# Eight start addresses, 64 bytes apart, for the stationary operands of two neighbouring routed tiles

## The reference

```python
h = jnp.einsum('bct,bcd->bdt', x, weights[subjects]) + bias[subjects][:, :, None]
h = h.reshape(-1, 512)                      # 4096 tokens
logits = h @ gate_weight.T                  # 16 experts in 4 groups of 4
# the best 2 groups, in them the best 4 experts; weights normalised, times 2.5
def body(acc, inp):
    g, u, d, we = inp                       # g, u: (256, 512)   d: (512, 256)
    y = silu(h @ g.T) * (h @ u.T) @ d.T
    return (acc + we[:, None] * y, None)
out, _ = jax.lax.scan(body, jnp.zeros_like(h), (gate_proj, up_proj, down_proj, cw.T))
shared = silu(h @ shared_gate.T) * (h @ shared_up.T) @ shared_down.T
return x + (out + shared).reshape(64, 64, 512)
```

## Time and profile before

| | us |
|---|---|
| median of 3 runs | 827.67 |
| lowest and highest run | 824.30, 828.04 |
| span of the profiled execution, first to last instruction | 823.5 |
| TensorE busy in it (4133 matmuls) | 811.2 |
| TensorE's share of the chain that ended last | 93% |

### The profile page before, as it was taken

One profiled execution on the slowest core, in us unless ns is written; L12 is line 12 of the kernel. 1 busy time (PEld: TensorE's weight loads), 2 busy tenths in 40 slices (PEclk: granted clock), 3 DMA queues, 4 the chain that ended last, 5 costly groups with the idle time before them and its releaser, 6 DMA issues.

```text
span 823.5 us, 19365 instructions
## 1 busy us (share of the span) xinstructions
PE 811.2 (99%) x4133; PEld 650.1 (79%) x4134; DVE 484.7 (59%) x1017; ACT 389.1 (47%) x782; POOL 434.8 (53%) x399
## 2 busy tenths in 40 slices
PE   9999999999999999999999999999999999999996
PEld 5567878888887788888888888888888888888874
DVE  5788899626544445644457446747557466464441
ACT  4864434435343445544346445546455355453441
POOL 5503111525567555566655655755665674765543
PEclk9999999999999999999999999999999999999999
DMA  8986967899999999899997999899998998998965
GB/s 301 395 320 176 249 148 220 221 219 270 235 251 233 182 188 190 189 286 239 185 198 187 280 216 206 209 264 187 244 264 170 285 245 203 235 207 176 194 80 69
DMA packets 145305, 181.52 MB, mean 220 GB/s; under 512 B 30570, under 2 KB 103922, under 8 KB 142834
## 3 DMA queue, kind: packets, MB, share of 16 engines
q0 software_dynamic: 37776, 89.08, 52.6%
q1 hardware_dynamic: 106528, 80.45, 37.8%
q10 hardware_dynamic: 834, 10.49, 3.7%
HBM read 82.52 MB, written 67.17 MB: 182 GB/s over the span
## 4 chain that ended last, share of the span: by engine, by line
PE 93%; DMA 3%; DVE 1%; issue 1%; ACT 0%; DVEq 0%; POOLq 0%; POOL 0%; SPq 0%; ACTq 0%
PE psGU L1111 47%; PE psY L1111 23%; PE psY L1169 5%; PE psH L982 4%; PE psGU L1152 4%; PE psGU L1154 4%; PE psGU L1153 4%; DMA x_ring<-x_pairs 2%; DMA raw_w<-ffn_w 1%; PE psT L982 1%; PE psM L1139 1%; PE psGU L1031 1%; PE psH L1008 0%; DMA cond_sb<-cond_w 0%; DVE split_w L1340 0%
## 5 line engine op out<-in xcount | busy, mean ns | idle before, releaser
L1111 PE MATMUL psGU<-split_w,xT_pair 128*128 x1716 | 414.2, 390 | 0.9 <-issue 0.9
L1111 PEld LDWEIGHTS psGU<-split_w,xT_pair 128*128 128x128 f32 x1716 | 321.8, 188 | 70.1 <-issue 1.8
L694 POOL DMA_INDIRECT out<-y_ring,idx_all x143 | 227.2, 1589 | 202.0 <-SPq L583 183.1
L1758 DVE SCALAR_TENSOR_TENSOR aT<-aT,w_ring,psGU 128x256 f32<-128x256 f32 x143 | 68.6, 480 | 238.0 <-ACT aT L934 217.3
L689 POOL DMA_INDIRECT tok_ring<-h_rows,idx_all x143 | 152.2, 1064 | 72.7 <-issue 42.1
L1111 PE MATMUL psY<-split_w,hidT_hi 128*128 x564 | 187.4, 413 | 0.0
L934 ACT ACTIVATE aT<-psGU 128x256 f32<-128x256 f32 x143 | 55.0, 385 | 253.9 <-PE psGU L1111 253.9
L840 ACT ACTIVATE y_ring<-psY 128x512 f32<-128x512 f32 x173 | 103.6, 599 | 99.7 <-PE psY L1111 62.3
L1111 PE MATMUL psY<-split_w,hidT_lo 128*128 x282 | 111.1, 394 | 0.0
L1111 PEld LDWEIGHTS psY<-split_w,hidT_hi 128*128 128x128 f32 x564 | 95.4, 189 | 12.6 <-issue 0.2
L1743 DVE STREAM_TRANSPOSE psT<-x_ring 128x512 f32<-128x512 f32 x143 | 102.6, 717 | 2.3 <-DMA w_ring<-tok_ring 2.3
(11 more groups left out here) (268 smaller groups left out, 652.8 us busy)
## 6 DMA issues: line engine op xcount, KB each, us to landing
x_ring<-tok_ring SPq DMA_DIRECT2D x284, 128.0 KB
raw_w<-ffn_w SPq DMA_DIRECT2D x17, 1536.0 KB, 9.8
out<-y_ring POOLq DMA_DIRECT2D x32, 256.0 KB, 10.6
x_ring<-x_pairs SPq DMA_DIRECT2D x12, 512.0 KB, 8.3
h_rows<-tok_ring SPq DMA_DIRECT2D x16, 256.0 KB, 9.6
h_rows<-y_ring SPq DMA_DIRECT2D x16, 256.0 KB, 10.4
tok_ring<-h_rows,idx_all POOLq DMA_INDIRECT x143, 6.3
out<-y_ring,idx_all POOLq DMA_INDIRECT x143, 6.0
```

Source lines behind the costliest of these rows:

```text
L694: pool.indirect_dma_start(out[:, :], bass.IndirectOffsetOnAxis(idx_all[:, r:r + 1], 0), y_ring[:, r % YRING, :], None, compute_op=ALU.add) ...
L1111: mm = pe.matmul(dst, a[:, slot, c], w(at + col + k * H), start=(k == 0 and a is high and at == 0), stop=(k == parts - 1 and a is low))
L1758: v.scalar_tensor_tensor(out=hid[:, half, :], in0=gate, scalar=w_ring[:, w_slot, bass.ds(expert, 1)], in1=up, op0=ALU.mult, op1=ALU.mult). ...
```

## The change

The slots of `xT_pair`, `hidT_hi` and `hidT_lo` get 16 unused numbers (64 bytes) behind them. A slot of `xT_pair` is then 2112 bytes apart from the next, a slot of `hidT_hi` and `hidT_lo` 1088 bytes. Four slots of `xT_pair` are 8448 bytes, 16 times 512 and 256 more; two of `hidT_hi` are 2176 bytes, 4 times 512 and 128 more. So the phases become

| operand | even tile | odd tile |
|---|---|---|
| `xT_hi` | 0 | 64 |
| `xT_lo` | 128 | 192 |
| `hidT_hi` | 256 | 320 |
| `hidT_lo` | 384 | 448 |

The moving operand of L1111 stays at phase 0. `y_ring` and all buffers behind it move by 512 bytes, and `entry` is cut from 9216 to 8192 bytes, so all phases of other buffers stay. Where the shared expert uses `hidT_hi` and `hidT_lo` as plain rows of 512 numbers, the access patterns become two pieces of 256 numbers. The number of matmuls, loads, copies, subtractions, transfers and waits is unchanged, and so is their order.

```diff
+SHIFT = 16
-        xT_pair = sb("xT_pair", [P, GROUP, H], F32R)
+        xT_pair = sb("xT_pair", [P, GROUP, H + SHIFT], F32R)[:, :, 0:H]
         xT_hi, xT_lo = xT_pair[:, 0:2, :], xT_pair[:, 2:4, :]
-        hidT_hi = sb("hidT_hi", [P, 2, I], F32R)
-        hidT_lo = sb("hidT_lo", [P, 2, I], F32R)
+        hidT_hi = sb("hidT_hi", [P, 2, I + SHIFT], F32R)[:, :, 0:I]
+        hidT_lo = sb("hidT_lo", [P, 2, I + SHIFT], F32R)[:, :, 0:I]
...
-        with nc.sbuf_tensor("entry_high", [P, ENTRY_RING * PAIRS * NRP // 2], F32R) as entry_high:
+        with nc.sbuf_tensor("entry_high", [P, GROUP * H], F32R) as entry_high:
             pass
-        entry_flat = sb("entry", [P, ENTRY_RING * PAIRS * NRP], F16)
+        entry_flat = sb("entry", [P, GROUP * H * 2], F16)
...
             if g % 2 == 0:
-                return xT_pair[:]
+                return xT_pair
...
         def shared_hid_high(g, c):
             if c == 1:
-                return hidT_lo[:].rearrange("p a i -> p (a i)")
+                return hidT_lo
             if g % 2 == 0:
-                return hidT_hi[:].rearrange("p a i -> p (a i)")
-            return tok_high[:, H + E:2 * H + E] if g == 1 else ties_low[:, H:2 * H]
+                return hidT_hi
+            return in_halves(tok_high[:, H + E:2 * H + E] if g == 1 else ties_low[:, H:2 * H])
+
+        def in_halves(ap):
+            return ap.rearrange("p (a i) -> p a i", a=2)
...
-                act.activation(shared_hid_high(g, c), shared_hid(g, c), ACT.Copy).then_inc(hidhi_ready, 2)
+                act.activation(shared_hid_high(g, c), in_halves(shared_hid(g, c)), ACT.Copy).then_inc(hidhi_ready, 2)
...
-                token = slice(j * P, (j + 1) * P)
+                pair, half = divmod(j, 2)
+                token = slice(half * P, (half + 1) * P)
                 for c in range(IK):
-                    low = shared_hid_low(g, c)
+                    low = in_halves(shared_hid_low(g, c))
...
-                        mm = pe.matmul(psY[n % 2][:], a[:, token], split_w[:, w:w + H], ...
+                        mm = pe.matmul(psY[n % 2][:], a[:, pair, token], split_w[:, w:w + H], ...
...
-                v.tensor_tensor(shared_hid_low(g, c), hid_c, shared_hid_high(g, c).bitcast(F32), ALU.subtract
-                                ).then_inc(hidT_ready, 2)
+                v.tensor_tensor(in_halves(shared_hid_low(g, c)), in_halves(hid_c), shared_hid_high(g, c).bitcast(F32),
+                                ALU.subtract).then_inc(hidT_ready, 2)
```

More of the change, by code:

```diff
@@ L1163, in shared_down @@
                     pe.wait_ge(y_ready, n - 1)
-                token = slice(j * P, (j + 1) * P)
+                pair, half = divmod(j, 2)
+                token = slice(half * P, (half + 1) * P)
                 for c in range(IK):
-                    low = shared_hid_low(g, c)
+                    low = in_halves(shared_hid_low(g, c))
                     for a, at in ((shared_hid_high(g, c), 0), (shared_hid_high(g, c), EW), (low, 0)):
                         w = at + UP + c * H
-                        mm = pe.matmul(psY[n % 2][:], a[:, token], split_w[:, w:w + H], start=(c == 0 and a is not low and at == 0),
+                        mm = pe.matmul(psY[n % 2][:], a[:, pair, token], split_w[:, w:w + H], start=(c == 0 and a is not low and at == 0),
                                        stop=(c == IK - 1 and a is low))
```

## The result

The changed kernel takes 833.25 us (median of 4 runs, 831.74 to 836.71), the kernel before 826.88 us (4 runs, 824.30 to 828.04). The ratio is 1.0095 with a 95% interval of 1.007 to 1.0119: slower by 6.4 us, where 9.6 us were forecast. The profiled spans are 829.9 and 823.5 us, the same 6.4 us apart.

A forecast was written before the change was run, and what follows sets the result against it. TensorE's step from matmul to matmul was taken as the bound; 8.2 us routed plus 1.0 and 0.4 us shared expert made 9.6 us, added to 827.67 for 837.2 us. The range was 826.5 to 842 us.

The forecast's parts named there:

- The bound: Whole kernel: TensorE, busy 99% of the span, sets the time through the step from one matmul to the next.
- Gate-up, routed: Routed tiles' gate-up product: twelve steps go from 2.73 to 2.784 us, 0.053 us more a tile.
- the mixed stretches: Four shared-expert stretches before the change with phases mixed: 232.0 ns a step, against 226.7 with all phases equal.
- Down, routed: Routed tiles' down product: steps already at 230 ns go to 232.0, about 0.004 us more a tile.
- Shared expert: Even groups: first products with `xT_pair` moving pay 1.0 us, down products 0.4 us; odd groups 0.
- Writes by ScalarE and VectorE: Copies to shifted places, some in two pieces: no cost to the time, as they lie under TensorE's work.
- The sum: Whole kernel: 8.2 us routed, 1.0 and 0.4 us shared expert, together 9.6 us slower.
- The distance from span to median: Whole kernel: the median of runs lies 4.2 us above the profiled span, kept for the changed kernel.
- The collision undone: Rival, routed long steps: unequal phases let loads arrive sooner, 17 us saved, about 810 us; chance of faster 0.14.
- No change: Rival: phases don't matter or steps settle; 827.7 to 829.1 us; chance 0.22, including shift not made and half case's lower end.
- The half case: Rival: only phase changes cost, one step in three stays at 226.7 ns; about 833 us, chance 0.08.

The follow-up runs named there:

- const64: Kernel before with all eight routed stationary operands at phase 64, moving operand at 0: 838.55 us against 825.92, ratio 1.0145.
- lo256: Kernel before with only the low x operands moved, to phase 256 in both tiles: 826.13 us against 827.22.
- allnear0: Kernel before with `ident`, `ties_low` and `entry_high` all moved to phase 0: ratio 0.9999 (0.9981 to 1.0017).
- odd64: Kernel before with only the x operands of odd tiles moved, high and low both to phase 64: 832.31 us against 825.92.
- lo128: Kernel before with only the low x operands moved, to phase 128 in both tiles: 834.81 us against 825.92.

## Why the prediction was right, and where it was not

**The bound.** Right. TensorE stays 99% busy, and the page after differ by 7.8 us of its busy time, and what moved is the step.

**Gate-up, routed.** Forecast 2.784 us for twelve steps, 0.053 more; measured 2.80 and 2.78, 0.06 more on average. The mean of the mixed stretches was a good price, for both tiles within 0.02 us. The reason given with it was wrong, though. "With phases that change from matmul to matmul they don't" settle is refuted by `const64` (no change, all steps long) and by `lo256` (change, steps as before). The mixed rows of before were mixtures with a difference at 64, 320, 352 or 256 to 448; for 320 and 352 `allnear0` shows that the difference did it. So it is partly luck that the price fitted: the change happened to bring differences that cost about as much as those in the mixed rows. For `lo256`, whose phases change from matmul to matmul too, the same reasoning would have forecast a loss that did not come.

**Down, routed.** Forecast 0.004 us more, measured 0.00: 1.60 us in both. Its steps are unsettled before the change, and those of 256 to 448 are no worse. At 64 they would be (`const64`, 0.02 us a tile).

**Shared expert.** Forecast 1.4 us, measured 0.9. The products with `xT_pair` moving behave as said in group 2 (5.56 us for 24, forecast 5.57). All the first products together gained 0.7 and not 1.0 us, because products behind a stall or a short matmul are unsettled in either kernel, and the down products of the even groups 0.15, not 0.4.

**Writes by ScalarE and VectorE.** Right: nothing. This includes the copies in two pieces, which the trace of before had only in one piece; groups of ACT by shape, changed kernel, then before:

```profile
L861 ACT ACTIVATE hidT_lo<-aT 128x512 fp32r<-128x512 f32 x8 | 5.1, 632 | 27.8 <-DVE aT L1702 27.8
L861 ACT ACTIVATE hidT_hi<-aT 128x512 fp32r<-128x512 f32 x4 | 2.5, 626 | 2.1 <-DVE aT L1702 2.1
```

```profile
L857 ACT ACTIVATE hidT_lo<-aT 128x512 fp32r<-128x512 f32 x8 | 5.1, 632 | 28.1 <-DVE aT L1697 28.1
L857 ACT ACTIVATE hidT_hi<-aT 128x512 fp32r<-128x512 f32 x4 | 2.5, 626 | 2.1 <-DVE aT L1697 2.1
```

**The sum.** 9.6 us forecast, 6.4 measured. Of the 3.2 us between them 1.9 are stalls at places that no phase touches, which the profiled execution of before had and I carried over unseen as if they would come again; 0.5 is the shared expert, 0.5 the head and the tail, and the rest is small: an undisturbed tile is 0.0565 us longer against 0.057 forecast, because two errors nearly cancel (gate-up paid a little more than forecast, down nothing instead of 0.004), and one tile's interval lies outside the 142. The distance from span to median was put at 4.2 us from three runs; the changed kernel's profiled execution took 831.74 us with a span of 829.9, 1.8 us apart, and with that the forecast would have been about 835.

**The rivals.** The collision undone is refuted for every difference tried: none gives twelve steps below 2.72 us, and none is clearly shorter than at 0, where load and stream begin alike. No change is refuted as well: `odd64` has 2.80 and 2.73 us for the same product in neighbouring tiles, apart in 64 bytes of phase alone. The Trainium skill has two independent read ports and a load that takes no bandwidth from the running matmul ("TensorE: Matmul & The Clock Gate", Part 2); by these runs the step depends all the same on where the two reads begin against each other. Its other rule, that TensorE waits on no one ("SBUF — State Buffer", Who interferes with whom), is about other engines, and these runs don't speak against it. No change, or nearly none, would probably have been the outcome had the spacing been 256 bytes. The half case has the measured time almost exactly, about 833 against 833.25, but it isn't what happened: it counted the routed tiles alone, with twelve steps in some 2.77 us, where 2.80 and 2.78 were measured, and that one step in three stays short is what `lo128` shows not to happen.

**What stays open.** Why a difference of 256 is harmless, 448 nearly so, and 64 or 384 not, and what makes a product at a difference of 16 settle or not. The load itself is recorded as 187 to 192 ns in all kernels; what gets longer is the time from its end to its matmul, 36 ns on average in the settled part of before's gate-up products and 43 in `const64`. The runs give the table, not the mechanism. Only float32r products with 128 stationary and 512 moving columns were measured, and each kernel was profiled once.

## What to carry to other kernels

When TensorE is the bound and its engine is always busy, divide distances between starts by the number of matmuls, and compare stretches of the same matmul with other operands: 5 ns on each of the 2574 long steps of the routed tiles are 12.9 us, 1.6% of this kernel. Before spreading operands over addresses, look for a place where the kernel already has both arrangements; here stretches of 24 matmuls of the shared expert gave the price of the change to within 0.02 us a tile. And try a constant shift beside a mixture, since the trace of before had only mixtures and could not say which of the two costs.

## What the runs showed of the hardware that I had not expected

- The step of float32r matmuls with 512 columns and a new stationary operand each depends on where the loaded operand begins against the streamed one. Over the twelve steps of a gate-up product it is 227.4 ns on average where they begin alike or 256 bytes apart (226.7 once settled), about 233 ns at differences of 32, 64, 128 and 384 bytes, and 228.7 at 448. A common shift, tried with 64 bytes, doesn't cost that.
- One load 128 bytes out of phase in three brings the average of all steps to 233 ns (`lo128`).
- Steps have a memory. Behind the transposes equal phases too need up to nine steps to come back to 226.7 ns (in the kernel before the longest case is five down steps and the first four of the next gate-up product), and its undisturbed tiles repeat in a row of seven, 4.320 to 4.354 us, to within a nanosecond.
- VectorE stands still for 3.8 to 5.9 us at about 265 us in all thirteen kernels, and in most of them again between 760 and 772 us, with no releaser in the profile. At these two places stops of 5.0 us and more cost TensorE 0.3 to 1.4 us, and those up to 4.8 us nothing. Elsewhere a shorter one went with a loss too: 4.44 us at 252 us in `allnear0`, with which TensorE lost 1.4 us.
